# A GRU scan on one core: r and c written by ScalarE into spare PSUM columns and read there by VectorE

## The reference, cut to what matters

```
def step(H, xs):                      # H: [32, 256], 256 steps, hidden size 256
    xz, xr, xh = xs                   # x projections of this step
    Z = sigmoid(xz + H @ Whz.T + bhz)
    R = sigmoid(xr + H @ Whr.T + bhr)
    H_tilda = tanh(xh + R * H @ Whh.T + bhh)
    H_new = Z * H + (1.0 - Z) * H_tilda
    Y = H_new @ Whq.T + bhq
    return H_new, Y
out = x + transpose(Ys)               # x: [32, 256 steps, 256]
```

## Time and profile before

| | us |
|---|---|
| median of 3 runs | 525.05 |
| lowest, highest | 524.43, 526.39 |
| the profiled execution's own time | 524.34 |
| its span, first to last instruction | 522.4 |
| granted TensorE clock | 1.000 of full |

### The profile page before, as it was taken

The page is one execution under the profiler, slowest core; times in us unless marked ns, Lnnn a source line. Parts: engine busy times, 40 slices in busy tenths (PEclk is TensorE's granted clock), DMA queues, the critical chain, the costliest instruction groups (busy, mean ns, idle before and its releaser), DMA issues.

```text
span 522.4 us, 96066 instructions
## 1 busy us (share of the span) xinstructions
PE 509.6 (98%) x44184; PEld 492.7 (94%) x44184; DVE 317.8 (61%) x1929; ACT 328.8 (63%) x1800; POOL 0.2 (0%) x4
## 2 busy tenths in 40 slices
PE   7499999999999999999999999999999999999997
PEld 7499999999999999999999999999999999999997
DVE  1266666666666666666666666666666666666665
ACT  2266666666666666666666666666666666666665
POOL 0000000000000000000000000000000000000000
PEclk9999999999999999999999999999999999999999
DMA  5111111111111121111121111111111111111111
GB/s 176 29 47 50 50 52 49 50 54 47 50 55 46 50 55 45 50 55 45 51 55 45 51 54 45 53 53 45 55 51 45 55 50 45 55 50 45 55 50 51
DMA packets 57735, 27.63 MB, mean 53 GB/s; under 512 B 6784, under 2 KB 56832, under 8 KB 57728
## 3 DMA queue, kind: packets, MB, share of 16 engines
q1 hardware_dynamic: 56880, 26.70, 18.3%
q10 hardware_dynamic: 848, 0.83, 0.5%
HBM read 18.98 MB, written 8.52 MB: 53 GB/s over the span
## 4 chain that ended last, share of the span: by engine, by line
PE 96%; issue 2%; DMA 1%; SPq 0%; DVE 0%; ACT 0%; ACTq 0%; DVEq 0%
PE r_ps L244 34%; PE c_ps L244 27%; PE z_ps L244 23%; PE y_ps L244 11%; DMA whq_sb<-in_whq_dram 1%; SPq L114 0%; SPq L115 0%; SPq L116 0%; SPq L112 0%; DVE u_sb L230 0%; DVE o_sb L212 0%; DVE h_sb L235 0%; ACT c_sb L189 0%; DVE rh_sb L225 0%; ACT r_sb L179 0%
## 5 line engine op out<-in xcount | busy, mean ns | idle before, releaser
L244 PE MATMUL c_ps<-xt_sb,wx_sb 128*32 128x64 f32 (+1 forms) x4104 | 172.1, 225 | 1.5 <-issue 1.5
L244 PE MATMUL z_ps<-xt_sb,wx_sb 128*32 128x64 f32 (+1 forms) x4104 | 163.9, 220 | 1.3 <-DMA wx_sb<-in_wx_dram 0.7
L179 ACT ACTIVATE r_sb<-r_ps 128x32 f32<-128x32 f32 x512 | 91.2, 198 | 106.2 <-PE r_ps L244 98.7
L225 DVE TENSOR_TENSOR rh_sb<-r_sb,h_sb 128x32 f32<-128x32 f32 x512 | 89.8, 193 | 86.3 <-ACT r_sb L179 81.9
L244 PE MATMUL z_ps<-h_sb,whz_sb 128*32 128x32 f32 x8192 | 124.1, 198 | 1.7 <-issue 1.7
L244 PE MATMUL c_ps<-rh_sb,whh_sb 128*32 128x32 f32 x8192 | 122.9, 198 | 2.4 <-issue 2.2
L244 PE MATMUL y_ps<-whq_sb,h_sb 128*32 128x128 f32 x2064 | 113.6, 279 | 0.3 <-DVE h_sb L235 0.3
L244 PEld LDWEIGHTS z_ps<-h_sb,whz_sb 128*32 128x32 f32 x8192 | 108.8, 111 | 1.8 <-issue 1.8
L244 PE MATMUL r_ps<-xt_sb,wx_sb 128*32 128x64 f32 (+1 forms) x4104 | 108.0, 219 | 0.0
L230 DVE SCALAR_TENSOR_TENSOR u_sb<-z_sb,c_sb 128x32 f32<-128x32 f32 x512 | 75.3, 189 | 53.6 <-ACT c_sb L189 53.6
L244 PEld LDWEIGHTS z_ps<-xt_sb,wx_sb 128*32 128x32 f32 (+1 forms) x4104 | 101.4, 111 | 1.6 <-issue 1.6
(11 more groups left out here) (27 smaller groups left out, 358.3 us busy)
## 6 DMA issues: line engine op xcount, KB each, us to landing
xt_sb<-in_xt_dram SPq DMA_DIRECT2D x130, 64.0 KB, 1.8
xres_sb<-in_xr_dram SPq DMA_DIRECT2D x130, 64.0 KB, 1.8
out_dram<-o_sb SPq DMA_DIRECT2D x130, 64.0 KB, 1.6
wx_sb<-in_wx_dram SPq DMA_DIRECT2D x3, 256.0 KB, 3.2
whr_sb<-in_whr_dram ACTq DMA_DIRECT2D x1, 256.0 KB, 5.1
whz_sb<-in_whz_dram ACTq DMA_DIRECT2D x1, 256.0 KB, 5.6
whh_sb<-in_whh_dram ACTq DMA_DIRECT2D x1, 256.0 KB, 6.0
whq_sb<-in_whq_dram SPq DMA_DIRECT2D x1, 256.0 KB, 7.0
```

What stands on the lines that cost most here:

```text
L179: nc.scalar.activation(r_sb[:, o], r_ps[:, o, here], ACT.Sigmoid).then_inc(s_r[o], 1)
L225: nc.vector.tensor_tensor(rh_sb[:, k], r_sb[:, k], old[:, k], ALU.mult).then_inc(s_rh[k], 1)
L244: return nc.tensor.matmul(ps, weights, moving, start=start, stop=False, skip_group_check=True, **kw)
```

## The change

ScalarE no longer writes r and c to SBUF tiles. r_sb and c_sb are gone, and the sigmoid and tanh write 32 columns from column 128 on (for one of the c halves from column 160) in banks of y_ps and z_ps. VectorE reads them there for rh (two halves) and u (two halves). The count of instructions on ScalarE and VectorE stays, and so do their shapes. TensorE's order and waits are the same.

The kernel lets no two engines use a bank at the same time, so waits change on ScalarE. In s = 1 steps, the second r half goes into the bank y_ps[p], which VectorE's residual reads; so the wait for s_res moves from the y seed to that second r sigmoid. The y seed now waits for the second rh half, and the z seed for the first u half (of which c lies in z_ps[p]).

```diff
+        spare = slice(P, P + B)
+        r_out = [[y_ps[1 - p][:, 0, spare], y_ps[p][:, 0, spare]] for p in range(2)]
+        c_out = [[z_ps[p][:, 0, spare], y_ps[p][:, 0, P + B:P + 2 * B]] for p in range(2)]
...
                     for o in range(K):
+                        if s == CS - 1 and o == K - 1:
+
+                            act.wait_ge(s_res, t + CS)
                         act.wait_ge(s_r_ps[o], t + 1)
-                        nc.scalar.activation(r_sb[:, o], r_ps[:, o, here], ACT.Sigmoid).then_inc(s_r[o], 1)
+                        nc.scalar.activation(r_out[p][o], r_ps[:, o, here], ACT.Sigmoid).then_inc(s_r[o], 1)
...
                     if s == CS - 1:
-                        act.wait_ge(s_res, t + CS)
+                        act.wait_ge(s_rh[K - 1], t + 1)
                         seed_y(p).then_inc(s_seed_y, CS)
                     for o in range(K):
                         act.wait_ge(s_c_ps[o], t + 1)
-                        nc.scalar.activation(c_sb[:, o], c_ps[:, o, here], ACT.Tanh).then_inc(s_c[o], 1)
+                        nc.scalar.activation(c_out[p][o], c_ps[:, o, here], ACT.Tanh).then_inc(s_c[o], 1)
...
                         seed(c_ps[:, :, W * p:W * p + W], N).then_inc(s_seed_c, CS)
+
+                        act.wait_ge(s_u[0], t + 2)
                         seed(z_view(p), Z).then_inc(s_seed_z, CS)
...
-                        nc.vector.tensor_tensor(rh_sb[:, k], r_sb[:, k], old[:, k], ALU.mult).then_inc(s_rh[k], 1)
+                        nc.vector.tensor_tensor(rh_sb[:, k], r_out[p][k], old[:, k], ALU.mult).then_inc(s_rh[k], 1)
...
-                        nc.vector.scalar_tensor_tensor(u_sb[:, k], z_sb[:, k], 1.0, c_sb[:, k],
+                        nc.vector.scalar_tensor_tensor(u_sb[:, k], z_sb[:, k], 1.0, c_out[p][k],
                                                        ALU.subtract, ALU.mult, reverse0=True).then_inc(s_u[k], 1)
```

More of the change, by code:

```diff
@@ L62, in gru_kernel @@
         h_sb = sb("h_sb", [P, K, SLOTS, B])
-        r_sb = sb("r_sb", [P, K, B])
         rh_sb = sb("rh_sb", [P, K, B])
@@ L66, in gru_kernel @@
         zh_sb = sb("zh_sb", [P, K, B])
-        c_sb = sb("c_sb", [P, K, B])
         u_sb = sb("u_sb", [P, K, B])
@@ L277, in _ @@
             warm.then_inc(s_warm, 1)
-            spare = y_ps[1][:, 0, 2 * P:2 * P + WCOLS]
+            other = y_ps[1][:, 0, 2 * P:2 * P + WCOLS]
             for n in range(ROUNDS):
                 for j in range(NQ):
-                    warm = mm(spare[B * j:B * j + B], ones_sb[:, B * j:B * j + B], ones_sb[:], start=True,
+                    warm = mm(other[B * j:B * j + B], ones_sb[:, B * j:B * j + B], ones_sb[:], start=True,
                               tile_position=(0, B * j))
```

## The result

The changed kernel takes 527.46 us (median of 10 runs, 526.39 to 528.81), the kernel before 525.32 beside it (10 runs, 524.24 to 526.79): 1.0044 times the time, interval 1.0031 to 1.0058. It is slower, by 2.1 us, and I had forecast 519.2. The time lies in the range that I gave, on the other side of the old one.

The account below looks back on a forecast made before the run. TensorE, busy 98% of the span, was taken to bound the kernel; 0.05 + 3 x 0.02 - 0.02 = 0.09 us a pass, times 64 is 5.8 us, gave 519.2 us, range 516.5 to 530.

Parts of the forecast that it names:

- TensorE bounds; the first load of a pass waits for the branch: Pass start: TensorE is busy 98% of the span; most of the 15.1 us wait stays, as the branch holds the load.
- 0.05 at the pass start: Pass start: TensorE's wait for the first new h goes when c comes earlier, gaining 0.05 us a pass.
- 0.02 for each c group at s = 0: Steps u = 0 and 2: the second rh comes 0.04 earlier, gaining the 0.02 us lost in each c block.
- VectorE 0 more: VectorE's rh and u: reading one operand from PSUM adds 0 ns, with ends of -2 and 98 ns.
- rival C: VectorE takes 60 ns longer reading PSUM, so rh and u come later: 0.22 us a pass lost, 539 us; chance 0.08.
- I take 40 ns saved: ScalarE's 32-column r and c from PSUM to PSUM: about 158 ns in place of 198; ends nothing and 50 saved.
- rival B: No change: ScalarE's saving is half, 20 ns, and u = 1 loses most of the gain: 524.5 us; chance 0.13.
- The seeds' new waits, nothing: The y seed's wait for the second rh and the z seed's for the first u cost nothing, being covered.
- The wait at u = 1: Second r sigmoid waits for the residual, starting at 255.72 in place of 255.66: -0.02 us, between +0.01 and -0.06.
- The wait at u = 3: Second r sigmoid: the residual ends before it starts, so the wait is over in time, gain 0.02 us.
- Rival A: Slower: PSUM destination saves nothing, and the residual wait makes the second r at u = 1 0.11 late: 532.0 us; chance 0.11.

Follow-up runs that it names:

- e5: Against the changed kernel: s = 1 residual moved behind both rh, y seed to the next step, no second wait at any r sigmoid; 520.78 us, 0.9912 times before.
- e6: Against the kernel before: only c goes to PSUM, r stays in SBUF, s_res waited for at the y seed; 524.62 us, 0.9978 times before.
- e8: Against the kernel before: only r goes to PSUM, except the second half of s = 1 steps; c in SBUF; 523.03 us, 0.9957 times before.
- e9: Kernel before plus, after its last residual, ScalarE sigmoids and VectorE products from SBUF or PSUM, each waiting for the previous; PSUM to PSUM sigmoid 182 ns.
- e2: Changed kernel with the second r sigmoid's two waits called in the other order, s_res count shifted by one; 524.96 us, 0.9999 times before.
- e1: Kernel before plus a long-met wait (s_bias), called first, ahead of the second r sigmoid in s = 1 steps; 531.21 us, 1.0116 times before.
- e7: Kernel before, writes still to SBUF, with the s_res wait moved to the second r sigmoid of s = 1, called last; 531.64 us, 1.0112 times before.

## Why the prediction was wrong, point by point

- **TensorE bounds; the first load of a pass waits for the branch.** Right: 15.9 us of wait are still there after the change, and 15.2 in e5.
- **0.05 at the pass start.** Right in place (e6), too large in size: 0.02 came.
- **0.02 for each c group at s = 0.** Right, place and size (0.29 to 0.27, e8): even a saving of 16 ns covers it.
- **VectorE 0 more.** Right: rh takes 191 ns where it took 193, and rival C fell with that. The Trainium skill (VectorE: DVE Perf Modes, "The TRN2 errata") would have 58 cycles from SBUF and 120 from PSUM. e9's 292 against 291 ns and 192 against 188 contradict it for this form.
- **The saving, "I take 40 ns saved". The mis-sized term: it measured 16.** I had taken the destination's saving from seeds whose source lies in SBUF, and put it on a sigmoid whose source lies in PSUM. e9 shows that the two savings overlap: 28 ns with the source in SBUF, 15 with it in PSUM. The range from 0 to 50 held it; rival B, with 20, was the case that came in this term, and e2, with the waits as B had priced them, measured 524.96 against B's 524.5.
- **The seeds' new waits, nothing.** Right: from the first record of r_ps<-zh_sb to the next step's first of r_ps<-u_sb, where a late c would show, it is 0.408 us at u = 1 in both kernels, and 0.453 and 0.454 at u = 3 (medians).
- **The wait at u = 1.** The start of the second r was forecast 0.22 behind the first, and it is 0.22. But this is chance: the price came from the separate instruction's wait for r_ps, not from the residual, for u = 3 shows the same 0.22 with the residual long over. The end is later than forecast, because the sigmoid is only 16 shorter: c lost 0.05, where I had 0.02, inside the bounds given for that step.
- **The wait at u = 3, "the wait is over in time, gain 0.02". This is the step that failed.** It lost 0.05. I had asked when s_res comes, and not what becomes of the other wait. The rows of ScalarE's order in the section on the change showed both waits at one instruction, and I priced only the one that was new. e1 shows the price without any late signal, and e2 and e7 that the step is free with the waits the other way round.

In one sum, with the measured pieces in the prediction's own form: 0.02 + 2 x 0.02 - 0.05 - 0.05 = -0.04 a pass against the +0.09 forecast. Of the 0.13 between, u = 3 makes 0.07, u = 1 0.03 and the pass start 0.03. The sign needed both errors. With the saving at 16 ns and the waits swapped the kernel is even with before (e2), so the size alone takes the forecast gain away and makes no loss. That the wait alone makes none either is only reckoned: with 40 ns saved the second r would end 0.02 late in both s = 1 steps, and 0.05 + 2 x 0.02 - 2 x 0.02 = 0.05 a pass would be left as gain. Rival A had the sign and the wait, but for another reason: it needed a saving of nothing and a residual that comes late, at u = 1 only.

Open: why the savings of source and destination overlap, and what the 45 ns between the wait record's end and the sigmoid's start are spent on; they are the same in the changed kernel, e1, e2 and e7 wherever the separate instruction holds the late signal. No run varied the number of waits at the sigmoid beyond two.

## What to carry to other kernels

An instruction with two waits has a separate wait instruction ahead of it, so ask of each added wait not only whether it is met in time but which signal then lands on the separate instruction. Here the signal that comes last had to be called first; better still is to move the other engine's work, as in e5, so that the instruction on the critical chain keeps one wait. A saving taken from a form with one side changed is not to be added to one with the other side changed: here the pair was worth 47 ns, the two apart 60.

## What the runs showed of the hardware that I had not expected

- A second wait that has long been met costs its ScalarE instruction 0.06 us if it is called first, so that the late signal stands on the separate instruction (e1: r pair 0.42 instead of 0.36): the 17 ns of that instruction's record and 45 behind it. Called last it costs nothing (e7, u = 3: 0.36; e2, u = 3: 0.34 with the shorter sigmoids).
- ScalarE's sigmoid of 32 columns: 229 ns from SBUF to SBUF, 201 SBUF to PSUM, 197 PSUM to SBUF, 182 PSUM to PSUM. The Trainium skill (ScalarE: Activation LUTs, "Step-by-step: what each stage is for") calls PSUM the destination with the lower latency, without a number; the runs agree, by 28 ns from SBUF and 15 from PSUM.
- VectorE's fp32 product of two operands takes as long with one of them in PSUM as with both in SBUF (e9: 188 and 192 ns with 32 columns, 291 and 292 with 128).
